# A ternary feed-forward phase: its loop written out and skewed by tile, with roundings and normalisation on ScalarE

## The reference

```python
def _weight_quant(w):
    scale = 1.0 / jnp.clip(jnp.mean(jnp.abs(w)), 1e-05)
    wq = jnp.clip(jnp.round(w * scale), -1.0, 1.0) / scale
...
def _act_quant(x):
    scale = 127.0 / jnp.clip(jnp.max(jnp.abs(x), axis=-1, keepdims=True), 1e-05)
    xq = jnp.clip(jnp.round(x * scale), -128.0, 127.0) / scale
...
def _bitlinear(x, w):
    return jnp.einsum('bsi,oi->bso', _act_quant(x), _weight_quant(w))
gate = jax.nn.silu(_bitlinear(x, w_gate))
up = _bitlinear(x, w_up)
return _bitlinear(gate * up, w_down)
...
x = x + _L1_ffn_ref(_layernorm(x, axis=-1), L1_ffn_w_gate, L1_ffn_w_up, L1_ffn_w_down)
```

## Time and profile before

| | us |
|---|---|
| median of three runs | 5296.53 |
| lowest and highest | 5285.67, 5299.82 |
| the profiled execution, its own time | 5291.64 |
| its span in the profile | 5289.7 |
| VectorE busy in the span | 3727.1 |
| TensorE busy in the span | 4856.2 |
| ScalarE busy in the span | 2862.9 |

### The profile page before, as it was taken

One profiled execution on the slowest core, in us unless ns is written; L12 is line 12 of the kernel. 1 busy time (PEld: TensorE's weight loads), 2 busy tenths in 40 slices (PEclk: granted clock), 3 DMA queues, 4 the chain that ended last, 5 costly groups with the idle time before them and its releaser, 6 DMA issues. The chain is left out here.

```text
span 5289.7 us, 71161 instructions
## 1 busy us (share of the span) xinstructions
PE 4856.2 (92%) x24012; PEld 2658.6 (50%) x24012; DVE 3727.1 (70%) x6699; ACT 2862.9 (54%) x6128; POOL 2533.2 (48%) x1463
## 2 busy tenths in 40 slices
PE   7899997799999798899889999999999999999955
PEld 5555555344444497344545555555555555555423
DVE  8666665688888587788656666666666666666588
ACT  5677773377777543567534454444544444444423
POOL 5555554100000241100157778777787777777700
PEclk9999998799999898899989999999999999999977
DMA  6566666553333005433543333333433333333100
GB/s 219 194 236 235 231 235 201 138 86 72 72 73 71 1 1 193 88 79 81 189 118 82 91 94 82 92 90 82 100 84 88 96 79 93 90 82 96 40 36 20
DMA packets 342979, 572.78 MB, mean 108 GB/s; under 512 B 48816, under 2 KB 142064, under 8 KB 341600
## 3 DMA queue, kind: packets, MB, share of 16 engines
q1 hardware_dynamic: 338976, 562.15, 39.3%
q10 hardware_dynamic: 3648, 6.17, 0.4%
HBM read 333.70 MB, written 200.28 MB: 101 GB/s over the span
## 5 line engine op out<-in xcount | busy, mean ns | idle before, releaser
L2744 POOL TENSOR_TENSOR la_acc<-la_acc,la_pr 128x1024 f32<-128x1024 f32 x704 | 1697.4, 2411 | 494.3 <-ACT la_pr L2702 458.9
L2702 ACT ACTIVATE la_pr<-la_s_ps 128x512 f32<-128x512 f32 x1536 | 794.0, 603 | 971.3 <-PE la_s_ps L2554 969.6
L2561 PE MATMUL la_o_ps<-la_pr,la_vf 128*64 128x512 f32 x3072 | 743.8, 605 | 0.0
L2553 PE MATMUL la_s_ps<-la_q_hl,la_k_hh 128*128 128x512 f32 x1536 | 690.2, 449 | 1.6 <-ACT la_q_hs L2678 1.3
L1825 DVE TENSOR_REDUCE ca_mx<-ca_m_ps 128x2 f32<-128x1024 f32 x512 | 600.7, 1217 | 123.2 <-PE ca_m_ps L1682 123.2
L1784 ACT ACTIVATE ca_pr<-ca_s_ps 128x512 f32<-128x512 f32 x1024 | 541.8, 601 | 204.2 <-PE ca_s_ps L1689 200.7
L2771 DVE TENSOR_REDUCE la_mx<-la_m_ps 128x2 f32<-128x1024 f32 x384 | 463.0, 1206 | 215.4 <-PE la_m_ps L2536 207.1
L2554 PE MATMUL la_s_ps<-la_q_hs,la_k_l 65*128 65x512 f32 x1536 | 609.1, 397 | 0.0
L2771 DVE TENSOR_REDUCE la_mx<-la_misc 128x2 f32<-128x1024 f32 x384 | 466.2, 1214 | 0.0
L2553 PEld LDWEIGHTS la_s_ps<-la_q_hl,la_k_hh 128*128 128x128 f32 x1536 | 290.0, 189 | 242.2 <-ACT la_pr L2702 102.6
L2561 PEld LDWEIGHTS la_o_ps<-la_pr,la_vf 128*64 128x64 f32 x3072 | 186.2, 136 | 346.7 <-issue 227.0
(11 more groups left out here) (400 smaller groups left out, 8745.6 us busy)
## 6 DMA issues: line engine op xcount, KB each, us to landing
la_k_hh<-scratch_k_high SPq DMA_DIRECT2D x128, 512.0 KB, 6.6
scratch_k_high<-sc_k_high SPq DMA_DIRECT2D x128, 256.0 KB, 2.6
scratch_k_low<-sc_k_low SPq DMA_DIRECT2D x128, 256.0 KB, 2.8
la_w_parts<-scratch_w_parts SPq DMA_DIRECT2D x64, 512.0 KB, 6.2
la_k_l<-scratch_k_low SPq DMA_DIRECT2D x64, 512.0 KB, 8.5
la_vf<-scratch_xv SPq DMA_DIRECT2D x64, 512.0 KB, 4.2
ca_ks<-scratch_k_rows SPq DMA_DIRECT2D x372, 64.0 KB, 3.5
scratch_vaug<-sc_v SPq DMA_DIRECT2D x16, 1024.0 KB, 4.4
```

Source lines behind the costliest of these rows:

```text
L2553: pe.matmul(s_ps[:, bank, :], k_hh[:, par, h, keys], q_hl[:, par, h, :], start=True, stop=False)
L2561: last = pe.matmul(o_ps[XD * h:XD * h + XD, :], vf[:, par, st, XD * h:XD * h + XD], pr[:, st % LAG, h, :], start=(st == 0), stop=(st == XT ...
L2702: act.activation(pr[:, st % LAG, h, :], s_ps[:, (2 * st + h) % 3, :], ACT.Exp, scale=scale).then_inc(p_done, 1)
L2744: pool.tensor_tensor(total, total, exps, ALU.add).then_inc(acc_done, 1)
```

## The change

Five things change, all in `ternary_ffn`:

1. All engines walk one written-out loop over the tiles, `for n in range(TILES + LAG)`, instead of the hardware loop. The token work stands at fixed slots of a batch (tile number modulo four): normalisation and maxima behind tile 0, integers behind tile 1, the turned tokens behind tile 3, the statistics of the batch after next behind tile 3. The down product and `finish` lag two tiles instead of one.
2. The first rounding pass of the hidden values (`round_hidden`) and of the tokens (`round_tokens`) goes from VectorE to ScalarE.
3. The normalisation of the tokens (`apply`) goes to ScalarE too, as scale and bias; GpSimd makes the bias (`shift`) in two further operations.
4. At the start the weight sums come ahead of the token maxima, the gate weights get their three passes first and alone, and TensorE begins when they are done. The first pass of up and down weights is on ScalarE.
5. The last batch is stored in four parts, one behind each tile.

```diff
@@ TensorE @@
-                def rest(b, par, it, has_next):
-                    for j in range(1, NT):
-                        gate_up(b, j)
-                        if j == NT - 1 and has_next:
-                            turn_tokens(b + 1)
-                        down(b, j - 1)
-                    if has_next:
-                        gate_up(b + 1, 0)
-                    down(b, NT - 1)
+                turn_tokens(0)
+                pe.wait_ge(w_done, 1)
+                gate(0)
+                pe.wait_ge(w_done, 2)
+                up(0)
+                for n in range(TILES + LAG):
+                    if n >= LAG:
...
+                        down(n - LAG)
+                    if n + 1 < TILES:
+                        gate(n + 1)
+                        up(n + 1)
+                    if 0 < n <= TILES:
+                        turn_hidden(n - 1)
+                    if of(n, INTEGERS) is not None:
+                        turn_tokens(of(n, INTEGERS))
@@ ScalarE @@
+                def apply(b):
+
+                    act.wait_ge(shift_done, b + 1)
+                    act.wait_ge(xstep, max(XSTEPS * (b - 1) + 1, 0))
+                    act.wait_ge(xround, NT * b)
+                    for j in range(NT):
+                        act.activation(xn[:, j, :], g.x[:, b * NT + j, :], ACT.Identity, bias=shift[:, j:j + 1],
+                                       scale=norm.rstd[:, j:j + 1]).then_inc(xn_done, 1)
...
+                def round_hidden(n):
+                    act.wait_ge(hstep, HSTEPS * n + 3)
+                    act.wait_ge(hq_done, n)
+                    act.activation(hr[:, :], h[:, n % 2, :], ACT.Identity, bias=round_c[:, 0:1],
+                                   scale=hinv[:, n % 2:n % 2 + 1]).then_inc(hr_done, 1)
...
+                act.wait_ge(constants_set, 2)
+                apply(0)
+                round_tokens(0)
+                keep_tokens(0)
+                act.wait_ge(setup, 7)
+                for i in range(1, 3):
+                    act.activation(raw[:, i, :], raw[:, i, :], ACT.Identity, bias=round_c[:, 0:1],
+                                   scale=winv[:, i:i + 1]).then_inc(w_rounded, 1)
+                gate(0)
+                for n in range(TILES + LAG):
+                    if 0 < n <= TILES:
+                        round_hidden(n - 1)
+                    if of(n, INTEGERS) is not None:
+                        round_tokens(of(n, INTEGERS))
+                    if of(n, TOKENS) is not None:
+                        keep_tokens(of(n, TOKENS))
+                    if n + 1 < TILES:
+                        gate(n + 1)
+                    if of(n, APPLY) is not None:
+                        apply(of(n, APPLY))
+                    if 0 < n <= TILES:
+                        keep_hidden(n - 1)
@@ VectorE @@
-                    dve.tensor_scalar(hr[:, :], hs, hinv[:, 0:1], ROUND, ALU.mult, ALU.add).then_inc(hr_done, 1)
...
-                    norm.apply(dve, b, lambda j: g.x[:, b * NT + j, :], lambda j: xn[:, j, :])
-                    dve.wait_ge(norm.normed, NT * b + NT)
+                def token_maxima(b):
+                    dve.wait_ge(xn_done, NT * (b + 1))
                     dve.tensor_reduce(amax[:, :], xn[:, :, :], AX.X, ALU.max, apply_absolute_value=True).then_inc(xstep, 1)
...
+                moments(0)
+                weight_sums()
+                token_maxima(0)
+                moments(1)
+                weight_means()
+                token_units(0)
+                token_integers(0)
+                for i in range(3):
+                    ternary(i)
+                for n in range(TILES + LAG):
+                    if n < TILES:
+                        hidden(n)
+                    if n >= LAG:
+                        finish(n - LAG)
+                    if 0 < n <= TILES:
+                        hidden_integers(n - 1)
+                    if n < TILES:
+                        hidden_units(n)
+                    if of(n, UNITS) is not None:
+                        token_maxima(of(n, UNITS))
+                        token_units(of(n, UNITS))
+                    if of(n, INTEGERS) is not None:
+                        token_integers(of(n, INTEGERS))
+                    if of(n, MOMENTS, 2) is not None:
+                        moments(of(n, MOMENTS, 2))
@@ SyncE @@
+                for n in range(TILES - NT, TILES):
+                    sp.wait_ge(x_done, n + 1)
+                    sp.dma_start(io["out"][B - 1][n % NT * P:(n % NT + 1) * P, :], g.x[:, n, :]).then_inc(out_stored, 16)
```

More of the change, by code:

```diff
@@ L2907, in turn_tokens, with gate, up, hidden @@
                     last.then_inc(tp_ready, 1)
-                def gate_up(b, j):
-                    n = NT * b + j
-                    if j == 0:
-                        pe.wait_ge(xT_done, b + 1)
-                    for ps, w, ready, free in ((g_ps, w_gate, g_ready, gated_done), (u_ps, w_up, u_ready, h_done)):
-                        pe.wait_ge(free, n)
-                        for half in range(2):
-                            for k in range(KD):
-                                last = pe.matmul(ps[:, half, :], xqT[:, k, j * P:(j + 1) * P], w[:, k, half * T:(half + 1) * T],
-                                                 start=(k == 0), stop=(k == KD - 1))
-                        last.then_inc(ready, 1)
-                def down(b, j):
-                    n = NT * b + j
+                def gate(n):
+                    if n % NT == 0:
+                        pe.wait_ge(xT_done, n // NT + 1)
+                    pe.wait_ge(gated_done, n)
+                    hidden(n, g_ps, w_gate).then_inc(g_ready, 1)
+                def up(n):
+                    pe.wait_ge(h_done, n)
+                    hidden(n, u_ps, w_up).then_inc(u_ready, 1)
+                def hidden(n, ps, w):
+                    rows = slice(n % NT * P, n % NT * P + P)
+                    for half in range(2):
+                        for k in range(KD):
+                            last = pe.matmul(ps[:, half, :], xqT[:, k, rows], w[:, k, half * T:(half + 1) * T],
+                                             start=(k == 0), stop=(k == KD - 1))
+                    return last
+                def turn_hidden(n):
                     pe.wait_ge(hq_done, n + 1)
@@ L2972, in turn @@
                     act.activation(hqT[:, :, :], ht_ps[:, :, :], ACT.Copy).then_inc(hT_done, 1)
-                def first():
-                    keep_tokens(0)
-                    gate(0, 0, 0)
-                def rest(b, par, it, has_next):
-                    for j in range(1, NT):
-                        gate(b, par, j)
-                        if j == NT - 1 and has_next:
-                            keep_tokens(b + 1)
-                        turn(b, j - 1)
-                    if has_next:
-                        gate(b + 1, 1 - par, 0)
-                    turn(b, NT - 1)
@@ L2988, in _ @@
-                tiles(act, first, rest)
+                act.wait_ge(constants_set, 2)
[20 more added lines that the diff above has]
+                        keep_hidden(n - 1)
@@ L2990, in _ @@
             @block.gpsimd
             def _(pool):
-                with pool.Fori(0, B) as b:
+                pool.memset(zeros[:, :], 0.0).then_inc(constants_set, 1)
+                for b in range(B):
+                    if b:
+                        pool.wait_ge(xn_done, NT * b)
                     norm.on_gpsimd(pool, b, g)
+                    pool.wait_ge(norm.rstd_done, b + 1)
+                    pool.tensor_tensor(scaled[:, :], norm.mv[:, :, 0], norm.rstd[:, :], ALU.mult).then_inc(scaled_done, 1)
+                    pool.wait_ge(scaled_done, b + 1)
+                    pool.wait_ge(constants_set, 1)
+                    pool.tensor_tensor(shift[:, :], zeros[:, :], scaled[:, :], ALU.subtract).then_inc(shift_done, 1)
@@ L3016, in token_integers, with hidden @@
                 def token_integers(b):
[L3017 to L3020 removed]
+                    dve.wait_ge(xround, NT * (b + 1))
                     dve.wait_ge(tp_ready, b)
                     dve.tensor_scalar(xq[:, :, :], rnd[:, :, :], ROUND, QMAX, ALU.subtract, ALU.min).then_inc(xq_done, 1)
[L3024 to L3027 removed]
+                def hidden(n):
+                    b, j = divmod(n, NT)
+                    hs = h[:, n % 2, :]
@@ L3067, in weights @@
-                    for i in range(3):
-                        dve.tensor_scalar(wq[i][:, :], raw[:, i, :], 1.0, None, ALU.min).then_inc(w_done, 1)
-                def first():
-                    dve.memset(ones[:, :], 1.0).then_inc(setup, 1)
-                    dve.memset(asum[:, 3:4], 0.0).then_inc(setup, 1)
-                    moments(0)
-                    tokens(0, 0)
-                    token_integers(0)
-                    weights()
-                    token_units(0, 0)
-                    hidden(0, 0, 0)
@@ L3100, in _ @@
-                tiles(dve, first, rest)
+                        dve.wait_ge(setup, 8)
```

(6 more changed lines are left out.)

127 lines of the change are left out of this document (62 added, 65 removed).

## The result

| | before | after |
|---|---|---|
| median, us | 5293.74 (4 runs) | 5228.32 (4 runs) |
| profiled execution, us | 5291.64 | 5230.18 |
| its span | 5289.7 | 5228.3 |
| the phase, from the first memset of its own (`tf_ones`) to the end of the span | 264.7 | 203.1 |

The ratio is 0.988, with a 95% interval of 0.986 to 0.990.

What follows compares the result with a forecast made beforehand. VectorE was taken as the engine to relieve, though not full, with waits for TensorE or ScalarE. 28 tiles -38.9, start -4.1, end +1.4, store -0.4 summed to -42 us: 5250, range 5232 to 5266.

Steps and rivals of the forecast that it cites:

- The start: Start of the phase: first product at 5051.3 instead of 5055.38, -4.1 us.
- The end: Tiles 28 to 31, product of tile 28 to last L3048: 24.0 to 25.2 us against 23.2, +1.4.
- The store: Last store, a quarter as large, behind the last L3048: a small estimated gain, -0.4 us.
- Writing the loop out: Loops of the last phase: removed register operations are on no waiting engine, 0 us.
- the clock term: 28 tiles: TensorE's new idle gap can bring 1.2 GHz; 1.5 us a batch, between bounds 0 and 4.2.
- The slots: Batch order in the 28 tiles: token maxima and units taken behind tile 0, token roundings and integers behind tile 1.
- the 2.2 wait: Once a batch, VectorE waits 2.2 us before the token maxima for ScalarE's four normalisations.
- VectorE's own sum: 28 tiles: four bare tiles of 4.1 plus 4.3 token work, 20.7 us a batch.
- the first: Rival, 28 tiles: normalisation wait hidden, clock holds, VectorE alone sets 20.7 a batch; 5227 us, chance 0.13.
- The second: Rival, 28 tiles: TensorE-ScalarE loop binds part of each batch, 22.7 + 3.8 = 26.5; 5267 us, chance 0.15.
- The third and fourth: Rivals: clock at 1.2 GHz throughout, 5309 us, chance 0.03; waits of before return elsewhere, 28 a batch, 5281, chance 0.04.

Runs made afterwards that it cites:

- e11_after_again: The changed kernel, unedited, run again on the same chip as two other kernels; 5232.3 us, ratio 0.989 to before.
- e1_unrolled: The kernel before with only the batch loop of its last phase written out; 5287.5 us, ratio 0.999 to before.
- e2_slots: The changed kernel with token maxima and units behind tile 0 and token integers behind tile 1, instead of tiles 1 and 2; 5236.3 us, ratio 0.990 to before.
- e8_spread: The changed kernel with ScalarE's four normalisations spread: one ahead of the copy, one behind it, two behind the next hidden rounding; 5216.2 us, ratio 0.986 to before.

## Why the prediction fell short

The 28 tiles carry nearly all of the miss: 167.8 predicted, 149.0 measured, 18.8 us. The other terms:

- **The start**, -4.1: right. The phase's own first product came 4.2 earlier. Sums back to back with the loads' landings, ScalarE's two passes at 2.0 each and the table load behind them are all in the rows.
- **The end**, +1.4: right, +1.4 in the profiled execution; a bare tile in the end takes 4.33 to 4.34 (4.35), and the last down product came at 1.2 GHz, as allowed for. That the sum was met so closely is in part luck: the same kernel had +2.6 in e11_after_again.
- **The store**, -0.4: too small, measured -1.2.
- **Writing the loop out**, 0: right (e1_unrolled).

In the 28 tiles:

- **The step that failed is the clock term**, the "1.5" a batch between the bounds 0 and 4.2, 10.5 us in all. That TensorE would get a gap of some 2.9 behind ScalarE's run, and that 1.2 GHz could follow, was right: gaps of 2.6 to 2.8, spells of 1.9 us groups at some of them. The price was wrong. In the order I had followed it was 0, the lower bound, in the six batches with the gap (e2_slots), because the spell lay under VectorE's work; I had named this cover and then charged for what stays low behind it, without finding the instruction of VectorE that would wait. In the order as it is, it was 3.9 us: three batches at 1.2 to 1.4. The reason given for the size of the term, a rising busy share of TensorE, did not hold either: in batches at full clock it was 13.7 in 21.2, the 0.65 of before.
- **The slots were misread**, "the maxima stand directly behind tile 0 on VectorE". They stand a tile later, and the 2.2 wait was not there. e2_slots against after prices that at 6.9 us, the 3.9 of the clock in it. In place of that wait came the one before `finish`, 1.38: ScalarE's run delays the copy and so the down product. The prediction noted that "KEEP is behind the normalisations", for TensorE's gap, and did not follow it to `finish`.
- **VectorE's own sum**, 20.7 a batch, was near: 19.85 when it waits for nothing (e8_spread). A bare tile takes 3.97 to 4.0, not 4.1.

Put together: 10.5 for the clock and 6.9 for the slots are 17.4 of the 18.8; the remaining 1.4 are small prices (22.22 a batch in e2_slots instead of 22.7, less a first batch that gained less, having waits of 2.2 in a clock spell of its own).

Of the rivals, the first (the wait hidden, the clock held, 20.7 a batch, 5227) gives the measured time, but by its mechanism it did not happen: a wait was there and so were spells. That is luck: its 144.9 for the 28 tiles is 7.9 above the 137.0 that its mechanism takes where it came true, in e8_spread, and wait and spells in after cost 12.0. The second, a loop of TensorE and ScalarE as the bound, hardly came: the sign named for it, a wait of the product of tile 3 for SiLU behind matmuls of 1.9, is there in two batches, 0.36 each, where that rival had 3.8 in every batch. The third and fourth did not come; the waits of before did not return.

## What to carry to other kernels

Where engines run down fixed lists, a move to a slower engine can pay: what counts is the time of the engine that is waited for, and how long a run the other one puts into one place. 2 us in one piece ahead of a copy cost 12 us in 28 tiles, 3.9 of them with clock spells, the same work in pieces of 0.6 to 1.1 nothing. To price such a change, read the slots from the code or the printed order to the end of the chain, and charge a slower clock only where you can name the instruction on the busy engine that waits for it.
